# Experts picked from logits, one exponential for their shares, and the borders of the last attention and of its neighbours in another order

## The reference

```python
logits = xf @ router_w.T
routing = jax.nn.softmax(logits, axis=-1)
top_w, top_i = lax.top_k(routing, K)
top_w = top_w / jnp.sum(top_w, axis=-1, keepdims=True)
```

## Time and profile before

| what | value |
|---|---|
| runs of the kernel before | 866.54 us median of 3 (863.76 to 872.35) |
| the profiled execution, device time | 863.16 us |
| its span in the trace | 861.4 us |
| mean granted TensorE clock | 0.899 |
| busy: TensorE, its weight loads, VectorE, ScalarE, GpSimd | 685.0, 463.0, 492.8, 394.0, 303.9 us |
| instructions of these | 4528, 4528, 1420, 905, 456 |
| DMA | 68.70 MB, mean 80 GB/s |

### The profile page before, as it was taken

How to read it: one execution, slowest core, us unless ns; L and a number is a source line. 1 busy time by engine, 2 the same in 40 slices (tenths; PEclk the granted TensorE clock), 3 DMA queues, 4 the chain that set the end, 5 groups by cost and what they waited for, 6 DMA issues and landing times. The chain is left out here.

```text
span 861.4 us, 15064 instructions
## 1 busy us (share of the span) xinstructions
PE 685.0 (80%) x4528; PEld 463.0 (54%) x4528; DVE 492.8 (57%) x1420; ACT 394.0 (46%) x905; POOL 303.9 (35%) x456
## 2 busy tenths in 40 slices
PE   2787889899988777989677877567887676779998
PEld 1455665566655454656344544346666555546665
DVE  4677767776787326336557866254554445354443
ACT  4465554566665534545144553235653434222221
POOL 4444453443220442436266543725242612000000
PEclk9999998999999877999769987669988889589999
DMA  6254333233330011333543310013333100033332
GB/s 185 61 134 116 88 104 95 81 83 90 102 101 27 27 45 48 107 92 97 180 98 93 76 45 14 37 53 105 93 94 131 38 3 1 3 91 96 96 97 62
DMA packets 92854, 68.70 MB, mean 80 GB/s; under 512 B 9720, under 2 KB 84344, under 8 KB 92424
## 3 DMA queue, kind: packets, MB, share of 16 engines
q1 hardware_dynamic: 88680, 59.34, 25.0%
q0 software_dynamic: 4096, 8.40, 3.1%
HBM read 30.94 MB, written 14.35 MB: 53 GB/s over the span
## 5 line engine op out<-in xcount | busy, mean ns | idle before, releaser
L968 DVE TENSOR_REDUCE negmax<-ps 128x2 f32<-128x512 f32 x256 | 169.6, 686 | 95.5 <-PE ps L2017 94.7
L1708 ACT ACTIVATE exps<-ps 128x512 f32<-128x512 f32 x256 | 148.5, 598 | 113.7 <-PE ps L2029 97.3
L2017 PE MATMUL ps<-stack 96*128 96x256 bf16 x512 | 103.3, 296 | 33.0 <-DVE negmax L968 21.5
L2029 PE MATMUL ps<-stack 99*128 99x256 bf16 x512 | 101.5, 289 | 17.8 <-DMA stack<-maxt 15.6
L1565 POOL DMA_INDIRECT gathered<-z,placed x64 | 62.5, 976 | 89.3 <-DVE placed L1237 45.8
L1583 POOL DMA_INDIRECT late<-outputs_moe,placed x64 | 62.2, 973 | 67.4 <-DMA outputs_moe<-y_kept 31.3
L2311 PE MATMUL ps<-pack_moe,gated 128*128 x184 | 82.0, 530 | 0.0
L2017 PEld LDWEIGHTS ps<-stack 96*128 96x128 bf16 x512 | 47.5, 103 | 59.5 <-DVE negmax L968 38.8
L2045 PE MATMUL ps<-exps,values 128*32 128x256 f32 x1024 | 75.9, 416 | 1.3 <-ACT exps L1708 1.3
L2029 PEld LDWEIGHTS ps<-stack 99*128 99x128 bf16 x512 | 44.4, 102 | 60.2 <-issue 23.5
L2327 PE MATMUL ps<-pack_moe,ht 128*128 x368 | 63.7, 298 | 8.4 <-DVE y_kept L1348 4.8
(11 more groups left out here) (218 smaller groups left out, 1303.2 us busy)
## 6 DMA issues: line engine op xcount, KB each, us to landing
stack<-qk_parts SPq DMA_DIRECT2D x168, 128.0 KB
stack<-weights_t SPq DMA_DIRECT2D x32, 256.0 KB, 3.2
outputs_moe<-y_kept SPq DMA_DIRECT2D x92, 64.0 KB
ht<-gathered SPq DMA_DIRECT2D x44, 128.0 KB, 2.4
pack_moe<-in_moe SPq DMA_DIRECT2D x11, 256.5 KB, 4.0
pack_moe<-in_moe SPq DMA_DIRECT2D x1, 2577.0 KB
gathered<-y_kept SPq DMA_DIRECT2D x10, 256.0 KB, 4.0
pack_moe<-in_moe SPq DMA_DIRECT2D x1, 1732.0 KB
```

Of the source, the lines that this page charges most:

```text
L968: dve.tensor_reduce(negmax_of[b % 2][:, :, h:h + 1].rearrange("p t h -> p (t h)"), ps[:, h % 2, :].rearrange("p (t k) -> p t k", t=2), AX, ...
L1708: nc.scalar.activation(exps[:, i, :], ps[:, 2 + h % 2, :], ACT.Exp, scale=scale)\
L2017: last = pe.matmul(ps[:, h % 2, t * T:(t + 1) * T], st[0:MAXROW, h, 0, t * P:(t + 1) * P], st[0:MAXROW, h, 1, :], start=True, stop=True)
L2029: last = pe.matmul(ps[:, 2 + h % 2, t * T:(t + 1) * T], st[0:MAXROW + 3, h, 1, t * P:(t + 1) * P], st[0:MAXROW + 3, h, 0, :], start=True, ...
```

## The change

Routing of the sorted parts: the two experts are taken from the differences of the logits to their maximum (`pick_by_logit`, ten steps less in all), and the exponential is taken of the second one's difference alone, one value a token; the shares are 1/(1+e) and e/(1+e) (`take_shares`), made later, for part 1 just ahead of its first join, with ScalarE's exponential behind all tiles. A first Silu or Gelu on a scratch value stands ahead of the tiles. The tables of beats move with it, and the sends start two beats earlier. SyncE spreads the first batch of att2 behind the store of tile 41, and loads moe2's weights in six pieces behind the spreads of batches 1 to 6.

att3: the first turn of `ctx` stands in moe2's tile 40; maxima are taken in the step of their batch; joins come one step later; the turns of steps 3 and 5 stand at the step's end; the loop has eight steps, and the rest is written out. moe3's groups are 8 and 8 tiles; group 0 is normed in step 6, its logits stand between the averages of the last two batches, its picks between their additions. Group 1 is normed, routed and turned in the first block.

The diff, cut to its core (`spread_heads` holds the lines that stood at L751 to L766 unchanged; the helpers of `single_head` hold its former bodies):

```diff
-             "logits": (-1, 15), "top": (0, 1), "exp": (0, 2), "first": (0, 4), "second": (0, 6), "mark": (0, 8), "rank": (0, 9),
-             "place": (0, 11), "weigh": (1, 12), "load": (2, 6), "logits2": (3, 3)},
+             "logits": (-1, 15), "top": (0, 1), "pick": (0, 4), "mark": (0, 6), "exp": (0, 7), "rank": (0, 8),
+             "place": (0, 9), "weigh": (1, 12), "load": (2, 6), "logits2": (3, 3)},
...
-             "logits": (0, 2), "top": (0, 3), "exp": (0, 4), "first": (0, 5), "second": (0, 6), "mark": (0, 7), "rank": (1, 0),
-             "place": (1, 1), "weigh": (1, 3), "load": (2, 3), "logits2": (3, 7)}}
-SEND_FROM = {"moe1": 14, "moe2": 9}
+             "logits": (0, 2), "top": (0, 3), "pick": (0, 4), "mark": (0, 5), "exp": (0, 6), "rank": (0, 6),
+             "place": (0, 7), "weigh": (1, 3), "load": (2, 3), "logits2": (3, 7)}}
+SEND_FROM = {"moe1": 12, "moe2": 7}
...
-SORT_BEATS = {s: {"logits": -1, "top": -2, "exp": -1, "first": -1, "second": 0, "mark": 0, "rank": 0, "weigh": 1,
-                  "place": 2, "load": 3} for s in SORTED}
+SORT_BEATS = {s: {"logits": -2, "top": -2, "pick": -2, "mark": -2, "rank": -1, "place": 0, "load": 3} for s in SORTED}
...
-JOIN_STEPS = {0: (8,), 1: (9, 10, 11), 2: (12,), 3: (13, 14, 15)}
+JOIN_STEPS = {1: (8,), 2: (9, 10, 11), 3: (12,), 4: (13, 14, 15)}
...
-PIECES = {"moe1": 12}
+TAKEN_OUT = -1e30
+PIECES = {"moe1": 12, "moe2": 6}
+SLOTS_TILE = 41
...
 GROUPS = {"moe1": PART, "moe2": PART, "att3": tuple(range(t, t + BT) for t in range(0, NT, BT)),
-          "moe3": (range(0, NT - BT), range(NT - BT, NT))}
-ROUTE_STEPS = {"moe1": 41, "moe2": 42, "moe3": 17}
+          "moe3": (range(0, 2 * BT), range(2 * BT, NT))}
+ROUTE_STEPS = {"moe1": 33, "moe2": 33, "moe3": 17}
...
                         load_tile(s, j)
                     if j >= AHEAD:
                         store_output(s, j - AHEAD)
+                    if s == "moe1" and j - AHEAD == SLOTS_TILE:
+                        spread_heads(*EARLY)
+
...
+                    if valid(p) and (s, p) != EARLY:
+                        spread_heads(s, p)
...
-                    if (s, p) == EARLY:
-
+                    if flow == "att2" and 1 <= p <= PIECES["moe2"]:
                         wait(sp, "y_psum", "moe1", 0)
-                        sp.dma_start(pack["moe2"][:, 0:cols["moe2"]], args["moe2"]).then_inc(loaded["moe2"], 16)
+                        load_piece("moe2", p - 1)
...
-            spread(0, NBLK - 2)
+            spread(0, 1)
...
                 if blk == 1:
-                    spread(NBLK - 1, NBLK - 1)
-                if blk == NBLK - 1:
+                    spread(2, NBLK - 1)
+                if blk == 2:
...
-                    if sort_at(nxt, "first", tail, u):
-                        route_pick(nxt, 0, (0,))
-                    if sort_at(nxt, "second", tail, u):
-                        route_pick(nxt, 0, (1,))
+                    if sort_at(nxt, "pick", tail, u):
+                        pick_by_logit(nxt, 0)
...
-                        route_weights(nxt, 0)
                         place_tokens(nxt, 0, 2)
+                        take_shares(nxt, 0)
...
+                for step in range(B):
                     p, m, d = step, step - 1, step - 2
                     if step == 0:
                         apply_all(s, 1, GROUPS[s][1])
...
+                    if step in (3, 5):
+                        stats_all(s, step // 2 + 1, GROUPS[s][step // 2 + 1])
                     if step >= 3 and 2 * (step - 3) in GROUPS["moe3"][0]:
...
-                        if step == B:
+                        if step == 6:
                             last.then_inc(sem["stats_taken"], 1)
-                    if step == B:
+                    if step == 6:
                         moments_all("moe3", 0, GROUPS["moe3"][0])
...
+                        average(d)
...
+                        take_sum(m)
+                    for t in JOIN_STEPS.get(step, ()):
+                        join_outputs("moe2", t)
+                    if step in (3, 5):
                         apply_all(s, step // 2 + 1, GROUPS[s][step // 2 + 1])
...
+                    take_max(p)
                     if valid(d):
+                        add_output(d)
+                    if step == 6:
                         apply_all("moe3", 0, GROUPS["moe3"][0])
+                average(B - 2)
+                take_sum(B - 1)
+                average(B - 1)
+                route_logits("moe3", 0)
+                add_output(B - 2)
+                route_pick("moe3", 0, (0,))
+                add_output(B - 1)
+                route_pick("moe3", 0, (1,))
+                route_weights("moe3", 0)
...
+            def pick_by_logit(s, g):
+
+
+                chain, over, idx, lgg, rtg, rsg, wg = router_of(s, g)
+                wait(dve, "route_exp_in", s, 0, g)
+                chain(dve.scalar_tensor_tensor(out=rtg[1], in0=rtg[0], scalar=0.0, in1=idx, op0=ALU.is_equal, op1=ALU.mult))
+                chain(dve.tensor_reduce(rsg[2], rtg[1], AX, ALU.min))
+                chain(dve.tensor_tensor(rtg[2], over(rsg[2]), idx, ALU.is_equal))
+                chain(dve.scalar_tensor_tensor(out=rtg[0], in0=rtg[2], scalar=TAKEN_OUT, in1=rtg[0], op0=ALU.mult, op1=ALU.add))
+                chain(dve.tensor_reduce(rsg[1], rtg[0], AX, ALU.max))
+                chain(dve.tensor_tensor(rtg[1], rtg[0], over(rsg[1]), ALU.is_equal))
+                chain(dve.tensor_tensor(rtg[1], rtg[1], idx, ALU.mult))
+                chain(dve.tensor_reduce(rsg[2], rtg[1], AX, ALU.min))
+                chain(dve.tensor_tensor(rtg[1], over(rsg[2]), idx, ALU.is_equal))
+
+            def take_shares(s, g):
+
+
+                chain, over, idx, lgg, rtg, rsg, wg = router_of(s, g)
+                ts = slice(GROUPS[s][g][0], GROUPS[s][g][-1] + 1)
+                wait(dve, "route_exp", s, 0, g)
+                chain(dve.tensor_scalar(rsg[0], rsg[3], 1.0, None, ALU.add))
+                chain(dve.reciprocal(share[:, 0, ts], rsg[0]))
+                chain(dve.tensor_tensor(share[:, 1, ts], rsg[3], share[:, 0, ts], ALU.mult))
+
...
                     chain(dve.tensor_tensor(full[:, 2, :], full[:, 0, :], full[:, 1, :], ALU.add))
...
                     chain(dve.tensor_tensor(ends, full[:, 2, :].unsqueeze(1).to_broadcast([P, TILES[g], E]),
...
+                if t == GROUPS[s][1][0]:
+                    take_shares(s, 1)
...
-                if e == 1:
+                if e == 0:
+                    apply_all(s, 1, GROUPS[s][1])
+                if e == 3:
                     route_logits(s, 1)
-                if e == 3:
+                if e == 4:
                     route_pick(s, 1)
-                if e == 4:
+                if e == 5:
                     route_weights(s, 1)
+
...
-                route_weights(s, 0)
                 stats_all(s, 1, GROUPS[s][1])
-                apply_all(s, 1, GROUPS[s][1])
                 for blk in range(NBLK):
                     for i in range(E + 1):
                         if i >= 1:
...
             def route_exp(s, g):
                 ts = slice(GROUPS[s][g][0], GROUPS[s][g][-1] + 1)
+                if s in SORTED:
+                    wait(act, "picked", s, 0, g)
+                    nc.scalar.activation(rs[3][:, ts], rs[1][:, ts], ACT.Exp).then_inc(sem["route_exp"], 1)
+                    return
...
                 if e == 0:
-                    for i in range(NBLK - 1):
-                        copy_weights(s, i)
-                    copy_all(s, range(3, 4))
-                if e == 2:
+                    copy_weights(s, 0)
+                    copy_weights(s, 1)
+                if e == 1:
+                    copy_all(s, range(2, 4))
+                if e == 3:
                     route_exp(s, 1)
-                if e == 5:
-                    copy_weights(s, NBLK - 1)
+                if e == 6:
+                    copy_weights(s, 2)
+                    copy_weights(s, 3)
...
+                    if p in (3, 5):
+                        copy_all(s, [p // 2 + 1])
+                        copy_context(p // 2 + 1)
+                copy_pt(B - 2)
+                take_exp(B - 1)
+                copy_all("moe3", range(2))
+                copy_pt(B - 1)
+                copy_ot(B - 2)
+                route_exp("moe3", 0)
+                copy_ot(B - 1)
+                nc.scalar.activation(nbias[:, 0:1], neghalf[:, 0, 0:1], ACT.Silu)
...
             def sorted_tiles(s):
...
+                nc.scalar.activation(nbias[:, 0:1], neghalf[:, 0, 0:1], ACT.Silu if s == "moe1" else ACT.Gelu)
...
...
                 if e == 0:
-                    for i in range(NBLK - 1):
-                        turn_weights(s, i)
-                    turn_all(s, range(3, 4))
+                    turn_weights(s, 0)
+                    turn_weights(s, 1)
                 if e == 1:
-                    wait(pe, "wt_ready", s, 0, NBLK - 2)
+                    turn_all(s, range(2, 4))
```

(20 more changed lines are left out.)

360 lines of the change are left out of this document (167 added, 193 removed).

## The result

| what | before | after |
|---|---|---|
| runs of one comparison, median | 868.19 us (4: 863.76 to 872.35) | 832.63 us (4: 830.04 to 834.89) |
| the profiled execution, device time | 863.16 us | 834.89 us |
| its span | 861.4 us | 833.1 us |
| mean granted TensorE clock | 0.899 | 0.912 |

The ratio is 0.9612, 95% interval 0.9575 to 0.965: 35.6 us faster. The forecast was 837.0, its own range 831 to 843. The two traces differ by 28.3 us, against a sum of 26.8. In the comparisons further down, one of the six runs of e6 took 914 us and one of its kernel before 3354 us, and the readings do not rest on these two.

What follows compares the result with a forecast made beforehand. The prediction took TensorE's own work (80% busy) plus the borders between layers as the bound. Six terms summed to 26.8 us, taken from 863.2 to 836.4, stated as 837; own range 831 to 843, wider range 822 to 856.

Steps and rivals of the forecast that it cites:

- Start of att2: Where att2 begins: early spread of batch 0 and weights in pieces gain 6.8 us, ends 5.2 and 8.5.
- First wait: Start of att2: TensorE's 5.21 us wait for batch 0's spread goes, 5.2 us gained.
- second wait: Start of att2: TensorE's 3.31 us idle before batch 1 goes once the weight load is cut in pieces.
- First tiles of moe1: Table loads leave the first tiles of moe1 and picks need no exponential: gain 1.5 us, ends 0 and 4.8.
- Border before moe2: End of att2 to moe2's first tiles: earlier sends and shorter routing gain 3.5 us, ends 1.2 and 5.
- att3's steps: Start and steps of att3: earlier start, joins and statistics out from between scores and exponential; gain 7.3 us, ends 4 and 10.
- End of att3: att3's end to moe3's first routed expert: interleaved batches, eight tiles normed earlier; gain 10.6 us, ends 5 and 14.
- First block: First block of moe3: takes over norm turns, router matmuls, weight turns and longer picks; loss 2.9 us, ends 0 and 5.
- the clock comes back: Rival, four low-clock stretches: shorter gaps keep full clock, some 11 us more go, 826 us; chance 0.17.
- The end is worth half: Rival, att3's steps and end: late hand-overs between interleaved engines leave 9 us instead of 17.9, 846 us; chance 0.24.
- grow with the pieces: Rival, att2's steps: weight pieces lengthen six steps by 6.7 us each, 877 us, slower; chance 0.03.
- given back: Rival, att3: it waits for gathers or instruction loading, only att2's start pays, 855 to 860 us; chance 0.08.

Runs made afterwards that it cites:

- e6: Changed kernel with att3's maxima taken again at the start of the next step, joins and statistics left as changed: 837.9 us, ratio 0.9651.
- e11: Kernel before with only the start of att2 changed (early spread of batch 0, moe2's weights in six pieces): 858.2 us, ratio 0.9926.
- e3: Changed kernel with batch 0's spread again behind all stores of moe1, moe2's weights still in pieces: 806.9 us, ratio 0.9629.
- e2: Changed kernel with moe2's weights again in one load, batch 0's spread still early: 805.3 us, ratio 0.9609.
- e5: Kernel before repeated, nothing edited: 866.8 us, ratio 0.9992.
- e10: Changed kernel with marks, ranks, places and sends of moe1's and moe2's first part at the old, later beats: 831.2 us, ratio 0.9612.
- e12: Changed kernel with e8's edit, and in att3's step 1 batch 0's exponential ahead of the copies of turned inputs: 828.3 us, ratio 0.9572.
- e4: Changed kernel without the early Silu and Gelu, part 1's exponential again beside the first tiles of moe1 and moe2: 808.5 us, ratio 0.963.
- e1: Changed kernel repeated, nothing edited, on a chip where before took 838.2 us: 803.0 us, ratio 0.9574.
- e9: Changed kernel with e6's late maxima, and the joins again behind the addition of a batch's output: 833.2 us, ratio 0.9638.
- e8: Changed kernel with moe3's group 1 normed and turned ahead of the first expert, its routing and weight turns spread out: 829.8 us, ratio 0.9576.

## Why the prediction was right, and where it was not

The forecast held, and most of its mechanism with it; part of the agreement in the total is luck. The sum of 26.8 taken from the median of 866.5 gives 839.7. The forecast said 837 without a term for the other 2.7, and the runs gained 35.6.

1. Start of att2, 6.8: measured 6.9, in e11 too. First wait, second wait and what is late next came as said (5.4 and 1.5 of it). The two edits aren't a plain sum, though. From moe1's last output to the first column matmul pass 20.6 us with neither (before), 19.0 with the pieces alone (e3), 17.7 with the early spread alone (e2) and 13.6 with both: 1.5 and 2.8 apart, 6.9 together. For the pieces the prediction names no cost, and e2 and e11 show none.
2. First tiles of moe1, 1.5: this term was mis-sized. The pair shows 4.1, and other traces say the same: 98.0, 98.4 and 96.6 us from last z to last output without the change (before, e5, e11), 91.6 to 93.9 with it (after, e6 to e10, e12). Of the 4.1, e4 gives 2.1 to the three table loads; its first output comes 2.3 later, where the forecast had 1.1 for all edits together. Most of the rest fits VectorE's placing operations, which stood between the first and the third output in the kernel before (4.9 us from one to the other, 3.3 after, 3.0 in e4); no run takes these alone. The same place explains most of the 2.4 in moe2 behind its first output, which the forecast left at nothing beside the 0.7 that it counted into term 3: 5.2 us from first to third output before, 3.3 after. No table load stood there in the kernel before.
3. Border before moe2, 3.5: 3.0 in the pair. The router's matmuls hold TensorE, as said, and e10 shows that the sends' two beats bring at most 0.5 through them. By what is left the border gained its time from routing and tables; e10 took neither back, and e4 put two more loads there than the kernel before had. The size was near, part of its reason was not.
4. att3's steps, 7.3: 8.5, but in other places. The start came 2.3 us early (2.0). The first two steps, taken as unchanged, went from 14.1 to 9.8 us: step 0's matmuls ran at 0.60 us instead of 1.22, at the high level, with no idle time before them. The six others went from 48.5 to 46.6, not 42.3: a stop of 3.7 us and a low stretch of the clock stood in steps 2 and 3; steps 4 to 7 are as forecast. On the chip without stops the six take 42.6, 42.2 and 42.0 us in e2 to e4 (44.3 in e1), so there the forecast's 42.3 came true. The reason given was right in its mechanism: work of VectorE between scores and maximum holds the exponential and with it TensorE (2.56 us in step 4 before, 1.43 in step 7 of e6). But maxima in their own step are only one of several edits that take it out: e6 takes them back for 2.0 us, as the joins and statistics had moved too, and e9 another 1.3 with the joins.
5. End of att3, 10.6: 11.5. Its 15.4 to the weights was 15.7 with the last operation in it. From the weights to the first expert it took 8.4 us, shorter than the 9.4 to 9.6.
6. First block, -2.9: -3.9. The wait for the picks (1.1) and for the first of two weight copies (0.8, forecast 0.6) stand in TensorE's row; e8 takes them and the turns out.

What no term held: -2.0 ahead of moe1 and -2.4 in att2's steps. The first stands in att0, which the change doesn't touch: the projections at 46.4 us (L2136) took 1.22 us, in before at the same place 0.70 (L2085), though the granted clock reads 1.00 there in both traces; why is open. The second is a stretch of low clock in batch 5's step, 14.6 us at a mean clock of 0.77 where before had 12.0 at 1.00. e1 has neither. They offset gains that the forecast missed (2.6 in moe1, 2.4 in moe2, 1.2 in att3, 0.9 at its end), so that the pair's 28.3 is nearer to the 26.8 than the parts are: that is luck.

Of the rivals, "the clock comes back" came true in part only: at three of the four borders the clock rose by 0.04 to 0.12, at the start of att2 it fell by 0.02. "The end is worth half" asks for under 9 from parts 4 and 5, which gave 20.0. The steps did not grow with the pieces (e2, e11), and nothing was given back.

## What to carry to other kernels

A table load between tiles of a pipeline in which ScalarE hands over every tile can stand on the path: three of them cost 2.1 us in one layer here and 5.0 in another. Put one use of the function ahead, where the engine idles, and take other functions out of the stretch. Small operations between two hand-overs do the same on VectorE. When several pieces of work share one place with some room, taking one of them back can show little or no loss in the step that you look at: look at every step, and test the pieces together before calling one of them the cause. An engine's queue that ends earlier brings little while other work holds the next engine, so look at what that engine does when the result lands.

## What was not expected of the hardware

Chips differ by 30 us on one kernel (803.0 and 832.6 changed, 838.2 and 868.2 before). On the slower ones ScalarE and VectorE, and TensorE behind them, stop for up to 6 us at a time, with the wait ended by something "remote"; a wait of ScalarE of 9.2 us at the end of att2 in e5 (9.1 in e11) is the longest. GpSimd stops at most of these places too, but goes on with its gathers during the one in att3. On the faster chip there is no such stop. They don't fall at random: all ten traces with stops have one behind 3 or 4 outputs of moe1, but for that of e9, one behind 12 or 13 and one behind 26 or 27; the same three places come again in moe2 (behind 3 or 4, 11 or 12, 26 or 27, with e10 lacking the first), and each has one at the end of att2. So these stops hang on the place in the program and on the chip, and not on the edits; only the one of ScalarE in att3 came with the changed kernels. The page counts nearly the same instruction transfers on both chips (39 and 40 packets in the first trace, 39 and 39 in e1), so what stops the engines stays open.

The clock's low stretches move between executions of like kernels: att2's steps took 66.4 and 66.0 us in the two traces of before, and 64.1 to 69.6 in those of changed kernels.
